# Four PSUM banks shared by both kinds of matmul tile, and a rebuilt prologue, in a graph-attention layer

## The reference, cut to what matters

```python
h = relu(layernorm(x, axis=-1))                 # x: (32, 512, 1024), batch, channel, node
q = einsum('c,bcn->bn', wq, h);  k = einsum('c,bcn->bn', wk, h)
s = q[:, None, :] + k[:, :, None]               # 1024 x 1024 per batch
att = softmax(where(s > 0, s, 0.01 * s), axis=-1)
agg = einsum('bcn,bmn->bcm', h, att)
out = x + relu(einsum('oc,bcm->bom', adj, agg) + bm[None, :, None])
```

## Time and profile before

| | us |
|---|---|
| median of 3 runs (2135.05 to 2136.04) | 2135.54 |
| profiled execution, its own time | 2132.22 |
| its span | 2130.5 |
| TensorE matmul busy | 2057.9 (97%) |
| VectorE busy | 1646.2 (77%) |
| ScalarE busy | 1220.8 (57%) |
| mean granted TensorE clock | 0.994 |

### The profile page before, as it was taken

How to read it: one execution, slowest core, us unless ns; L and a number is a source line. 1 busy time by engine, 2 the same in 40 slices (tenths; PEclk the granted TensorE clock), 3 DMA queues, 4 the chain that set the end, 5 groups by cost and what they waited for, 6 DMA issues and landing times.

```text
span 2130.5 us, 35177 instructions
## 1 busy us (share of the span) xinstructions
PE 2057.9 (97%) x11312; PEld 958.5 (45%) x11312; DVE 1646.2 (77%) x3661; ACT 1220.8 (57%) x1873; POOL 398.2 (19%) x266
## 2 busy tenths in 40 slices
PE   4599999999999999999999999999999999999999
PEld 2244444444444444444444444444444444444444
DVE  6877788778788777787777887787887777877753
ACT  3655555655556665556655556555566555566543
POOL 0012221112211122212122211122111222121221
PEclk9799999999999999999999999999999999999999
DMA  5255544555534565444555444555445554445441
GB/s 168 98 141 145 138 104 128 135 144 138 132 91 149 129 153 138 103 115 143 137 154 132 101 123 137 142 138 128 96 146 129 153 138 102 117 143 138 114 100 40
DMA packets 178625, 271.51 MB, mean 127 GB/s; under 512 B 87649, under 2 KB 87649, under 8 KB 170337
## 3 DMA queue, kind: packets, MB, share of 16 engines
q1 hardware_dynamic: 178528, 270.59, 48.6%
HBM read 202.91 MB, written 67.63 MB: 127 GB/s over the span
## 4 chain that ended last, share of the span: by engine, by line
PE 89%; DVE 4%; issue 3%; ACT 2%; DMA 1%; SPq 0%; DVEq 0%; POOLq 0%; ACTq 0%
PE acc L332 19%; PE acc L333 19%; PE acc L334 19%; PE vps L316 10%; PE vps L317 10%; PE vps L318 10%; PE small L302 2%; DVE p_ring L626 1%; DVE p_lo L633 1%; DVE den_out L606 1%; ACT y L427 1%; DMA ab_rows<-ab_col 1%; DMA wm_nat<-in_adj_dram 0%; DVE v_lo L638 0%; ACT v_hi L420 0%
## 5 line engine op out<-in xcount | busy, mean ns | idle before, releaser
L332 PE MATMUL acc<-p_hi,v_hi 128*128 128x512 f16 x2048 | 777.9, 380 | 17.8 <-ACT y L427 17.8
L333 PE MATMUL acc<-p_lo,v_hi 128*128 128x512 f16 x2048 | 777.3, 380 | 0.0
L334 PE MATMUL acc<-p_hi,v_lo 128*128 128x512 f16 x2048 | 777.2, 379 | 0.0
L730 POOL TENSOR_TENSOR res<-res,y 128x512 f32<-128x512 f32 x256 | 393.7, 1538 | 1711.9 <-ACT y L427 1711.9
L408 ACT ACTIVATE p_ring<-ab_row,cols 128x512 f32<-128x512 f32 x512 | 349.5, 692 | 170.5 <-DVE p_lo L633 155.2
L626 DVE SCALAR_TENSOR_TENSOR p_ring<-ab_row,cols,p_ring 128x512 f32<-128x512 f32 x512 | 376.7, 747 | 64.5 <-ACT p_ring L408 35.3
L316 PE MATMUL vps<-wmT_hi,h_hi 128*128 128x512 f16 x1024 | 388.8, 380 | 0.9 <-DVE v_lo L638 0.9
L317 PE MATMUL vps<-wmT_lo,h_hi 128*128 128x512 f16 x1024 | 388.8, 380 | 0.0
L318 PE MATMUL vps<-wmT_hi,h_lo 128*128 128x512 f16 x1024 | 388.6, 379 | 0.0
L606 DVE SCALAR_TENSOR_TENSOR den_out<-den_row,cols 128x512 f32<-128x512 f32 x512 | 376.3, 771 | 0.0
L633 DVE SCALAR_TENSOR_TENSOR p_lo<-p_ring,p_hi 128x512 f16<-128x512 f32 x512 | 349.0, 682 | 5.3 <-ACT p_hi L416 5.1
(11 more groups left out here) (60 smaller groups left out, 782.6 us busy)
## 6 DMA issues: line engine op xcount, KB each, us to landing
xs<-in_x_dram SPq DMA_DIRECT2D x128, 512.0 KB, 6.0
res<-in_x_dram SPq DMA_DIRECT2D x256, 256.0 KB, 3.4
out_dram<-res SPq DMA_DIRECT2D x256, 256.0 KB, 2.4
den_row<-den_rows SPq DMA_DIRECT2D x32, 1024.0 KB, 4.6
ab_row<-ab_rows SPq DMA_DIRECT2D x32, 1024.0 KB, 6.8
wm_nat<-in_adj_dram SPq DMA_DIRECT2D x1, 1024.0 KB, 9.3
den_rows<-cols SPq DMA_DIRECT2D x32, 8.0 KB, 1.6
ab_rows<-ab_col SPq DMA_DIRECT2D x32, 8.0 KB
```

The lines of the kernel that those rows point to most:

```text
L332: pe.matmul(ps[:, :], v_hi[:, nt, chans], p_hi[:, hf, nt, :], start=(nt == 0), stop=False)
L333: pe.matmul(ps[:, :], v_hi[:, nt, chans], p_lo[:, hf, nt, :], start=False, stop=False)
L334: mm = pe.matmul(ps[:, :], v_lo[:, nt, chans], p_hi[:, hf, nt, :], start=False, stop=(nt == NT - 1))
L730: pool.tensor_tensor(res[:, k, :], res[:, k, :], y[:, k % 2, :], ALU.add).then_inc(s_add, 1)
```

## The change

The two `vps` and two `acc` banks become four `mix` banks: V tile nt uses bank nt mod 4, unit k bank k mod 4. Units 0 to 3 now wait for `v_lower` of V tiles 4 to 7 of their own batch, units 4 to 7 for the relu four units back; V tiles 0 to 3 wait for relus 4 to 7, V tiles 4 to 7 for `v_lower` four tiles back.

In the prologue the weights are loaded on ScalarE's queue, adj before the small column loads; x of second goes into the residual tile `res`; x of (1,0) is loaded as soon as first's h is made. VectorE makes two of first's four `h32`. First's denominator rows and `ab_row` are spread by 16 TensorE transposes each into the ring banks and `small`, then copied. Second's h, q, k, exponentials and denominators move from the prologue into the period of first, where no denominators are mixed with the p tiles any more. There second's `ab_row` goes out at store 6 and comes back at store 7, behind the x loads of (1,1).

```diff
+        mix = [bank(f"mix{i}") for i in range(MIX)]
+        first_rows = ring + [small]
...
@@ sync, prologue
+                sp.dma_start(xs[:, c, :], channels(first, c)).then_inc(s_x[c], 16)
             for c in range(CT):
+                sp.dma_start(x_second[:, c, :], channels(second, c)).then_inc(s_x1[c], 16)
+            sp.wait_ge(s_hhi, CT)
+            sp.wait_ge(s_h32, CT)
+            for c in range(CT):
+                sp.dma_start(xs[:, c, :], channels((1, 0), c)).then_inc(s_x[c], 16)
             for k in range(U):
+                sp.wait_ge(s_h32, CT + k // 2 + 1)
                 load_residual(first, k)
...
             def period(b, one, two, three):
+                late = 3 if at(b, first) else 0
                 store(b, 0)
                 for k in range(1, U):
                     store(b, k)
                     if one:
                         load_residual(nxt(b), k - 1)
-                        if k == 3:
+                        if k == 3 + late:
                             write_ab_rows(nxt(b))
-                        if k == 4:
+                        if k == 4 + late:
                             load_ab_rows(nxt(b))
                     if three and k == 6:
                         for c in range(CT):
                             load_x(nxt(b, 3), c)
...
@@ tensor
+            def spread_first(columns, done):
+                for r in range(2):
+                    for t in range(NT):
+                        dst = first_rows[2 * r + t // 4]
+                        mm = pe.transpose(dst[:, (t % 4) * P:(t % 4 + 1) * P],
+                                          columns[:, r, t:t + 1].to_broadcast([P, P]), ident[:, :])
+                mm.then_inc(done, 1)
...
             def v_tile(b, nt):
-                wait(pe, s_vlo[nt % 2], cnt(b, NT // 2, nt // 2))
+                if nt < MIX:
+                    wait(pe, s_y[nt % 2], cnt(b, U // 2, (nt + MIX) // 2 + 1 - U // 2))
+                else:
+                    pe.wait_ge(s_vlo[nt % 2], cnt(b, NT // 2, (nt - MIX) // 2 + 1))
...
             def unit(b, k, midway=None):
-                wait(pe, s_y[k % 2], cnt(b, U // 2, k // 2))
+                if k < MIX:
+                    pe.wait_ge(s_vlo[k % 2], cnt(b, NT // 2, (k + MIX) // 2 + 1))
+                else:
+                    pe.wait_ge(s_y[k % 2], cnt(b, U // 2, (k - MIX) // 2 + 1))
                 for nt in range(NT):
+                    if midway and nt == 3:
+                        midway(second)
...
                 for k in range(U):
-                    unit(b, k)
+                    if at(b, first) and k == 4:
+                        project_qk(second)
+                    unit(b, k, spread_qmax if at(b, first) and k == 4 else None)
                 if one:
+                    step = 5 if at(b, first) else 2
                     for nt in range(NT):
-                        if two and nt == 2:
+                        if two and nt == step:
                             project_qk(nxt(b, 2))
-                        if two and nt == 5:
+                        if two and nt == min(step + 3, NT - 1):
                             spread_qmax(nxt(b, 2))
                         v_tile(nxt(b), nt)
...
@@ tensor, prologue
+            v_tile(first, 0)
+            pe.wait_ge(s_exp, 1)
+            spread_first(cols[:, 0, 0:2, :], s_d1)
+            for nt in range(1, NT):
                 v_tile(first, nt)
-            project_qk(second)
-            spread_qmax(second)
+            pe.wait_ge(s_dn, D_OPS)
+            spread_first(ab_col, s_a1)
...
@@ scalar, period of first
+                if at(b, first):
+                    normalise(second, 0)
+                    normalise(second, 1)
+                    relu(b, 0)
+                    normalise(second, 2)
+                    normalise(second, 3)
+                    after = {0: 1, 3: 2}
...
+                    if at(b, first) and nt == 5:
+                        exponentials(second)
                 relu(b, 3)
                 relu(b, 4)
+                if at(b, first):
+                    for k in range(5, U):
+                        relu(b, k)
+                    for ct in range(CT):
+                        normalise(nxt(b, 2), ct)
+                        v_upper(nxt(b), ct)
+                    v_slots(nxt(b), two, CT)
+                    return
...
@@ scalar, prologue
+                for i, w in enumerate((wq, wk)):
+                    act.dma_start(wqk_row[:, i, :], w.partition_broadcast(P)).then_inc(s_wv, 16)
+                act.dma_start(wm_nat[:, :, :], adj.rearrange("(t p) c -> p t c", p=P)).then_inc(s_w, 16)
+                    for i, w in enumerate((wq, wk)):
+                        act.dma_start(wqk_col[:, i, :], w.rearrange("(t p) -> p t", p=P)).then_inc(s_wv, 16)
+                    act.dma_start(bias_o[:, :], bm.rearrange("(t p) -> p t", p=P)).then_inc(s_wv, 16)
...
@@ vector
+            def first_period(b):
+                for ct in range(CT):
+                    h_lower(second, ct)
+                weight(b, NT)
+                for nt in range(NT):
+                    if nt < NT - 1:
+                        weight(b, NT + nt + 1)
+                    p_lower(b, NT + nt)
+                    if nt == 1:
+                        q_head(second)
+                    if nt == 4:
+                        q_tail(second)
+                for nt in range(NT):
+                    denominator(second, nt)
+                row_scales(second)
+                for ct in range(CT):
+                    statistics(nxt(b, 2), ct)
+                normaliser(nxt(b, 2))
+                for ct in range(CT):
+                    h_lower(nxt(b, 2), ct)
+                    v_lower(second, ct)
+                v_slots(second, True, CT)
...
+            for nt in range(NT):
+                denominator(first, nt)
+                v_lower(first, nt)
+            row_scales(first)
             statistics(second, 2)
             statistics(second, 3)
             normaliser(second)
+            copy_first_b(0)
+            copy_first_b(1)
```

More of the change, by code:

```diff
@@ L434, in v_slots @@
                 for nt in range(NT):
-                    v_upper(b, nt)
+                    if nt + ahead < NT:
+                        v_upper(b, nt + ahead)
                     p_upper(b, nt)
@@ L468, in period, with load_weights @@
                     v_slots(nxt(b), two)
+            def load_weights():
+                for i, w in enumerate((wq, wk)):
+                    act.dma_start(wqk_row[:, i, :], w.partition_broadcast(P)).then_inc(s_wv, 16)
+                act.dma_start(wm_nat[:, :, :], adj.rearrange("(t p) c -> p t c", p=P)).then_inc(s_w, 16)
+                with nc.allow_non_contiguous_dma(reason="512 weights and biases, once"):
+                    for i, w in enumerate((wq, wk)):
+                        act.dma_start(wqk_col[:, i, :], w.rearrange("(t p) -> p t", p=P)).then_inc(s_wv, 16)
+                    act.dma_start(bias_o[:, :], bm.rearrange("(t p) -> p t", p=P)).then_inc(s_wv, 16)
+            load_weights()
             absolute_sums()
             for ct in range(CT):
-                normalise(first, ct)
+                h_upper(first, ct)
+            for ct in range(2, CT):
+                h_full(first, ct)
             weights_upper()
             exponentials(first)
+            copy_first_den(0)
+            copy_first_den(1)
             for nt in range(NT):
                 v_upper(first, nt)
-            for ct in range(CT):
-                normalise(second, ct)
+            copy_first_a(0)
+            copy_first_a(1)
             leak(first, 0)
@@ L484, in _ @@
                     leak(first, nt + 2)
-                if nt == 3:
-                    exponentials(second)
             period((0, 0), True, True)
@@ L647, in v_slots @@
                         weight(b, nt + 1)
-                    v_lower(b, nt)
+                    if nt + ahead < NT:
+                        v_lower(b, nt + ahead)
                     p_lower(b, nt)
@@ L682, in _ @@
             q_tail(first)
-            v_lower(first, 0)
             statistics(second, 0)
             statistics(second, 1)
-            v_lower(first, 1)
+            for nt in range(NT):
+                denominator(first, nt)
+                v_lower(first, nt)
+            row_scales(first)
             statistics(second, 2)
             statistics(second, 3)
-            for nt in range(NT):
-                denominator(first, nt)
-                if nt < NT - 2:
-                    v_lower(first, nt + 2)
-            row_scales(first)
             normaliser(second)
-            for ct in range(CT):
-                h_lower(second, ct)
+            copy_first_b(0)
+            copy_first_b(1)
             weight(first, 0)
@@ L701, in _ @@
                 p_lower(first, nt)
-                if nt == 1:
-                    q_head(second)
-                if nt == 2:
-                    q_tail(second)
```

(2 more changed lines are left out.)

119 lines of the change are left out of this document (70 added, 49 removed).

## The result

| | before | after |
|---|---|---|
| median of 5 runs, us | 2135.54 (2134.88 to 2136.46) | 2146.44 (2144.42 to 2147.88) |
| ratio | | 1.0048, 95% interval 1.0036 to 1.0059 |
| profiled execution / its span | 2132.22 / 2130.5 | 2144.42 / 2142.7 |
| `project_qk` of (1,1), end of the head | 195.86 | 218.41 |
| from there to the end of the span | 1934.6 | 1924.3 |

The kernel is 0.5% slower. The last two rows hold the whole story: the part behind the head is 10.3 us shorter, the head 22.5 us longer, and 22.5 - 10.3 = 12.2 is the difference of the spans. The chain of waits gives both rows: `project_qk` stands in it once per batch, so it serves as a milepost.

A forecast was written before the change was run, and what follows sets the result against it. TensorE, with matmuls filling 97% of the span, was taken as the bound, so only its idle time or work counts. 14.2 us lost in the head less 8.3 gained in the loop put the median at 2141.4 us, range 2130.5 to 2150.

The forecast's parts named there:

- The loop: Four banks in the loop: 0.64 us gained in each of 13 iterations, 8.3 us in all (4.4 to 16.9).
- the new wait: Unit 4 in each loop iteration: TensorE stalls 0.8 us for the last p tile's `p_lo`.
- the old loss: Unit 2 in each loop iteration before: 1.44 us lost waiting for relu 0's bank, gone with four banks.
- The collision: In the loop, GpSimd's residual add holds a denominator pass off for about 1.0 us, making it 0.6 us late.
- The head: Prologue and period of first: 14.2 us lost at the end of the head.
- S: Prologue, start of ScalarE's first sums: forecast at 18 us, range 15 to 20.
- the load of `den_row`: Period of first, loading second's denominator rows: 4.6 us, after 0.3 + 1.6 for the write.
- 16 passes 10.7: Period of first: second's 16 denominator passes on VectorE take 10.7 us.
- row_scales 0.6: Period of first: `row_scales` takes 0.6 us after second's denominator passes.
- Faster: Rival, chance 0.17: small pieces pass x of second, S is 14, the head moves up 4.0; 2128.8 us.
- The change only moves the loop's wait: Rival, chance 0.15, slower: unit 4 loses all that unit 2 gains; 2149.7 us.
- No difference: Rival, chance 0.33: loop gain and head loss cancel within 4.3 us, if 16.9 gained or V tile 0 by 32.

The follow-up runs named there:

- e1: The kernel before with only the four shared banks, its prologue untouched: 2123.6 us, ratio 0.9950 to before.
- e4: The changed kernel with second's `ab_row` asked for ahead of the x loads of (1,1) and `spread_qmax` of (1,0) after V tile 7: 2138.8 us, ratio 1.0025 to before.
- e9: The changed kernel with SyncE's queue asking for second's x only after the weights (adj) have landed: 2141.2 us, ratio 1.0000 to before.
- e11: The changed kernel with e4's two reorderings, e9's wait and GpSimd's adds held behind the denominator passes: 2120.8 us, ratio 0.9912 to before.
- e12: The changed kernel with only GpSimd's adds held back (unit 5's in the period of first, unit 3's elsewhere): 2136.1 us, ratio 0.9985 to before.
- e5: e1's kernel with GpSimd's residual add of unit 3 held until VectorE's 16 denominator passes are made: 2114.0 us, ratio 0.9868 to before.
- e10: e7's kernel with e5's wait for GpSimd's add: 2103.5 us, ratio 0.9830 to before.
- e6: e1's kernel with first's a and b rows spread by TensorE in place of the trip over DRAM: 2121.1 us, ratio 0.9901 to before.
- e7: e6's kernel with second's normalisation (statistics and h) moved ahead of the first rows: 2112.4 us, ratio 0.9862 to before.
- e8: The changed kernel with the three small column loads first on ScalarE's queue: 2145.6 us, ratio 1.0022 to before.

## Why the prediction was right, and where its sizes were off

**The direction and the mechanism held.** Forecast were a gain in the loop and a larger loss in the head, net +5.9; measured +10.9, inside the range. Both sizes were too small, by 2.0 and by 8.3 us, so the loop hid a part of the error of the head. e1 shows the gain alone, and e4, e9, e11 and e12 shrink the loss where the text had placed it.

**The loop: 8.3 forecast, 10.3 measured.** Two periods in which nothing is lost take 127.74 us (twice 63.87, in every run). The 13 iterations average 129.33 before and 128.54 after: 1.59 us were lost in each, 0.80 are. The forecast had 1.44 and 0.8. So its term for the new wait was right, and the mis-sized term is the old loss. There was a second wait for relu, at unit 7, which I did not see. Before, in the iteration of the earlier trace rows:

```profile
377.73 0.76 ACT L427 ACTIVATE y<-acc,bias_o,unscale_o 128x512 f32<-128x512 f32 x1
378.20 0.38 PE L334 MATMUL acc<-p_hi,v_lo 128*128 128x512 f16 x1
378.54 0.39 PE L332 MATMUL acc<-p_hi,v_hi 128*128 128x512 f16 x1
```

Relu 5 stands behind two instructions for h on ScalarE, and unit 7 needs its bank: its first matmul was due at 378.42, 0.22 us after the last one, and started 0.12 late. The profile lists no idle time there, since a matmul's record is longer than the step to the next. In four banks unit 7 waits for relu 3 instead.

The new wait has the size that was forecast. The collision first: in all 13 iterations the pass that meets the add takes 1.39 to 1.41 us instead of 0.74, a hold of 0.66 where the forecast had 0.6. What varies is VectorE's idle time at the jump back. TensorE's wait is that time less 1.67 or 1.68 us in each of the 26 iterations of the changed kernel and e1. At the 2.25 us of the earlier trace rows that is 0.58 us of idle, and with the 0.16 us by which two records overlap, 0.74 lost, where I had rounded 366.75 - 365.97 to 0.8 (the sum that gives 365.97 comes to 366.01). The changed kernel's jumps average 2.30 us, those of e1 2.46, and so the same loop gained 10.3 us in one and 8.2 in the other. That difference is luck as far as the runs show; what sets the length of the jump is open.

**The collision itself.** I read 1.0 us off one collision and took it for the time that an add holds a pass off, counted from its start. The changed kernel has four more, GpSimd's add and the VectorE instruction that met it; the last pair is the one of the loop:

```profile
113.86 1.61 POOL L842 TENSOR_TENSOR res<-res,y 128x512 f32<-128x512 f32 x1 [3.91 <-ACT y L470]
119.04 1.47 POOL L842 TENSOR_TENSOR res<-res,y 128x512 f32<-128x512 f32 x1 [3.57 <-ACT y L470]
124.22 1.34 POOL L842 TENSOR_TENSOR res<-res,y 128x512 f32<-128x512 f32 x1 [3.71 <-ACT y L470]
386.11 1.27 POOL L842 TENSOR_TENSOR res<-res,y 128x512 f32<-128x512 f32 x1 [1.40 <-ACT y L470]
```
```profile
114.28 1.75 DVE L699 SCALAR_TENSOR_TENSOR den_out<-den_row,cols 128x512 f32<-128x512 f32 x1
119.32 1.74 DVE L699 SCALAR_TENSOR_TENSOR den_out<-den_row,cols 128x512 f32<-128x512 f32 x1
124.47 1.11 DVE L706 TENSOR_TENSOR den<-den_part 128x8 f32<-128x8 f32 x1
386.53 1.40 DVE L699 SCALAR_TENSOR_TENSOR den_out<-den_row,cols 128x512 f32<-128x512 f32 x1
```

Take from each VectorE instruction its own length (0.74 us for a pass, 0.17 for `den`): it really began at 115.29, 120.32, 125.41 and 387.19. The adds ended at 115.47, 120.51, 125.56 and 387.38. So the VectorE instruction waits until 0.15 to 0.19 us before the add's end, whatever of the add is left, and the earlier trace rows fit too (365.62 against 365.81). The add waits in the same way. Take 1.27 us, the length of an add that meets nothing, from the ends of the first three: they really began at 114.20, 119.24 and 124.29, 0.14 or 0.15 us before the pass ended that ran when they were recorded (114.35, 119.39, 124.43). The add of the earlier trace rows is such a one, held to 364.54 by the pass at 363.94. The one at 386.11 was recorded beside a `p_lower` and was not held; it kept the pass off until 1.08 us after its start. The Trainium skill, page "SBUF — State Buffer", section "SBUF: two separate sides", says that the two hold each other off for the whole instruction, whichever starts first. The trace agrees, but for the 0.14 to 0.19 us of overlap. Even an instruction of 8 columns is stretched, from 0.17 to 1.11 us.

**The head: 14.2 forecast, 22.5 measured.** The mileposts, forecast and measured:

| step | forecast | measured | late by |
|---|---|---|---|
| first sums of ScalarE, S | 18 | 19.6 | 1.6 |
| second's `project_qk` | 94.2 | 96.2 | 2.0 |
| denominators of second start | 108.5 | 111.6 | 3.1 |
| h of (1,0) starts | 127.6 | 133.8 | 6.2 |
| `ab_row` of second asked for | 139.5 | 145.8 | 6.3 |
| `spread_qmax` of (1,0) | 153.5 | 161.6 | 8.1 |

The differences of the last column are the mis-sized terms: the start +2.0, 1.6 of it at S; the load of `den_row`, 5.94 us where the earlier trace rows gave 4.6, which is the next +1.1 and 0.2 that was made up (two stores were issued right behind it; that they slowed it is not shown); then **+3.1 for collisions, the term that was missing**: I wrote "16 passes 10.7" where they took 12.87, and "row_scales 0.6" where `den` alone took 1.12. I had worked out the collision for the loop with care and never asked for it in the period of first, where the same adds meet passes that are no longer mixed with other work. e12 shows it: 10.8 us for the passes with the adds held back. Last, `ab_row` took 7.50 us where I had 5.8. From its landing to `spread_qmax` it was 8.3 us, as forecast (8.2).

**The rivals.** *Faster*, with the small pieces passing x of second: S was 19.6, not 14, so its condition failed. e9 sets S to 14.3 by other means: 5.3 us off S moved the milepost by 3.7. That is 0.7 for each us, where the rival (and my range) counted one for one, so its 4.0 was too high. The page "DMA: Bandwidth & Descriptors" of the Trainium skill, section "Queues, rings and completion order", lets the DMA engines take turns between queues. The trace agrees: with x of second on the other queue adj landed 14.6 us after its issue and the bias 15.2, with that load held back (e9) 12.1 and 9.8. *The change only moves the loop's wait* is refuted by e1. *No difference* had named a loop gain of up to 16.9 us; e5 reaches 17.7 in the rest (1934.6 - 1916.9), but only with the adds held back.

**What stays open.** The new prologue's head is 24.3 us longer than e1's (218.4 - 194.1); the 22.2 are that less the longer jumps of e1. e11's head takes back 16.2. It still ends 17.2 us behind e10's. In e11 VectorE stands idle 4.8 us for `den_row` of second and then makes 10.8 us of passes with no p tile between them; together 15.6, which would account for most of it, but no run mixed them again inside the changed prologue, so that is argued and not shown.

## What to carry to other kernels

Judge a bundle by its parts: here one half was worth 10 us and the other cost 22, and the net of +11 hid both. Before taking a slow trip away, look at what runs beside it; its gain comes only when that work is moved as well (e6 against e7). And where two engines hold each other off, as GpSimd's add and VectorE's passes do here, hold back the one that has time: a single wait on GpSimd was worth 9.5 us to TensorE.

## What the runs showed that I had not expected

- An issue can hold its engine. In the changed kernel the third 2 KB column load kept ScalarE's queue for 7.95 us (4.43 to 12.38), and its first work, a table load, came at 12.41. With less traffic on the other queue (e9) the hold was 5.71 us. On SyncE's queue before, the same load took 0.66 us to issue; in e8, ahead of the large loads, 0.53. What fills up is not shown.
- GpSimd's add and a two-input VectorE pass hold each other off in both directions, each until 0.14 to 0.19 us before the other's end. The wait shows as length: a pass of 0.74 us as 1.40 to 1.75, an add of 1.27 as 1.34 to 1.81.
- TensorE can lose 0.12 us at a wait for which the profile lists no idle time (unit 7, before). The step from one start to the next shows it.
- Three 2 KB loads of 512 scattered numbers landed 5.3, 8.4 and 12.3 us after their issue with nothing large ahead of them on their queue, while the other queue moved x (e8).
